# FP4 weight preparation with ScalarE's part in it, and a later place for the NF4 LoRA product

## The reference, cut to what matters

```python
def _lin_lora(x, W, A, B):            # NF4 block; W = NF4[codes] * scales per 64
    base = einsum('bsh,oh->bso', x, W)
    lora = einsum('bsr,or->bso', einsum('bsh,rh->bsr', x, A), B)
    return base + lora

def nvfp4_qdq(x, select_num):         # FP4 block; for w_gate, w_up, w_down and activations
    s = maximum(max(abs(x)) / (448.0 * 6.0), 1e-12)
    xb = (x / s).reshape(..., D // 16, 16)
    sb = clip(max(abs(xb), axis=-1) / 6.0, 1e-12, 448.0)
    a = xb / sb
    q = sign(a) * FP4_LEVELS[digitize(abs(a), FP4_BOUNDS)]   # 0, .5, 1, 1.5, 2, 3, 4, 6
    dq = (q * sb).reshape(x.shape) * s
    return where(arange(D) >= D - select_num, x, dq)         # the last 128 stay
```

## Time and profile before

| what | us |
|---|---|
| runs of the kernel | 823.1, 827.39, 827.72; median 827.39 |
| the profiled execution, its own time | 826.83 |
| its span | 825.5 |
| busy in the span: TensorE, VectorE, ScalarE, GpSimd | 725.4, 569.2, 443.6, 191.4 |
| mean granted TensorE clock | 0.957 |

### The profile page before, as it was taken

The page is one execution under the profiler, slowest core; times in us unless marked ns, Lnnn a source line. Parts: engine busy times, 40 slices in busy tenths (PEclk is TensorE's granted clock), DMA queues, the critical chain, the costliest instruction groups (busy, mean ns, idle before and its releaser), DMA issues.

```text
span 825.5 us, 11308 instructions
## 1 busy us (share of the span) xinstructions
PE 725.4 (88%) x4136; PEld 539.0 (65%) x4136; DVE 569.2 (69%) x1083; ACT 443.6 (54%) x575; POOL 191.4 (23%) x176
## 2 busy tenths in 40 slices
PE   2798765988999998889998998788999899959998
PEld 1565522656777766667665777576777688947886
DVE  4779966553597788879897986468463434477773
ACT  4778876556767767877765712255322211224542
POOL 0204000022263542534555444112201100000000
PEclk9999956999999999999998999999999999978999
DMA  7636688776366676758766111211301110200001
GB/s 280 223 107 216 206 260 266 234 246 197 125 200 205 200 240 208 227 170 265 231 178 186 65 38 43 57 28 50 90 0 36 36 52 10 77 1 13 25 26 39
DMA packets 56039, 110.55 MB, mean 134 GB/s; under 512 B 9888, under 2 KB 20800, under 8 KB 55984
## 3 DMA queue, kind: packets, MB, share of 16 engines
q1 hardware_dynamic: 42560, 78.43, 29.9%
q10 hardware_dynamic: 9040, 17.30, 6.4%
q0 software_dynamic: 4384, 14.09, 5.9%
HBM read 91.65 MB, written 18.15 MB: 133 GB/s over the span
## 4 chain that ended last, share of the span: by engine, by line
PE 52%; DVE 21%; ACT 10%; issue 9%; DMA 6%; SPq 1%; ACTq 1%; POOL 0%; DVEq 0%; POOLq 0%
PE bank L1130 13%; PE bank L1131 13%; PE bank L1132 13%; ACT hot L1537 3%; PE bank L1238 3%; DVE x L1906 2%; DVE hot L1783 2%; DMA wide_buf<-in_down_flat 2%; DVE bank L1809 2%; ACT c L1496 2%; PE bank L1426 2%; PE bank L1280 1%; PE bank L1251 1%; DVE q_a L1856 1%; DMA codes<-c 1%
## 5 line engine op out<-in xcount | busy, mean ns | idle before, releaser
L1537 ACT ACTIVATE hot<-rep,levels 128x2048 f16<-128x2048 f16 x96 | 193.6, 2057 | 18.2 <-ACT c L1496 11.1
L1130 PE MATMUL bank<-zt_h,w_h 128*128 128x512 f32 (+1 forms) x232 | 93.2, 402 | 2.5 <-DVE zt_l L1894 2.0
L1132 PE MATMUL bank<-zt_h,w_l 128*128 128x512 f32 (+1 forms) x232 | 91.3, 394 | 0.0
L1131 PE MATMUL bank<-zt_l,w_h 128*128 128x512 f32 (+1 forms) x232 | 91.2, 393 | 0.0
L1238 PE MATMUL bank<-hot,diag 128*32 128x512 f16 x1160 | 78.6, 401 | 2.2 <-ACT hot L1537 2.2
L1130 PE MATMUL bank<-w_h,xq_h 128*128 128x512 f32 (+1 forms) x192 | 74.4, 387 | 5.2 <-DVE w_l L1925 3.0
L1131 PE MATMUL bank<-w_l,xq_h 128*128 128x512 f32 (+1 forms) x192 | 72.0, 375 | 0.0
L1132 PE MATMUL bank<-w_h,xq_l 128*128 128x512 f32 (+1 forms) x192 | 71.9, 374 | 0.0
L2050 POOL TENSOR_TENSOR q_a<-q_a,q_m 128x384 f32<-128x384 f32 (+3 forms) x34 | 35.7, 1050 | 107.6 <-DVE q_m L1677 106.9
L2106 POOL TENSOR_TENSOR at_l<-ztok,at_h 128x512 fp32r<-128x512 f32 x28 | 37.4, 1336 | 80.8 <-ACT at_h L1569 80.7
L1238 PEld LDWEIGHTS bank<-hot,diag 128*32 128x32 f16 x1160 | 26.3, 99 | 45.6 <-issue 24.3
(11 more groups left out here) (222 smaller groups left out, 1688.8 us busy)
## 6 DMA issues: line engine op xcount, KB each, us to landing
rep<-codes SPq DMA_DIRECT2D x58, 512.0 KB
codes<-c SPq DMA_DIRECT2D x29, 256.0 KB
raw<-in_codes_gu_t ACTq DMA_DIRECT2D x14, 512.0 KB
sc<-in_scales_gu_t SPq DMA_DIRECT2D x56, 128.0 KB
raw<-in_codes_attn_t ACTq DMA_DIRECT2D x8, 512.0 KB
raw<-in_codes_down_t ACTq DMA_DIRECT2D x7, 512.0 KB
sc<-in_scales_down_t SPq DMA_DIRECT2D x28, 128.0 KB
wide_buf<-in_gate_flat SPq DMA_DIRECT2D x5, 512.0 KB, 4.5
```

The lines of the kernel that those rows point to most:

```text
L1130: PE.matmul(psum, lh, rh, start=first, stop=False, **kw)
L1131: PE.matmul(psum, lh, rl, start=False, stop=False, **kw)
L1132: return PE.matmul(psum, ll, rh, start=False, stop=last, **kw)
L1537: S.activation(hots[plan.slot[hot_ring(t), (t, m)]][:], codes_in_place(t), ACT.Relu, bias=bias, scale=slope).then_inc(sem("ramp_act"), 1)
```

## The change

In `make_plan`: for jobs after the attention ones, `lora(t-1)` is no longer emitted behind `look(t)` in step t, but first thing in step t+1, ahead of `high_part(t-1)`. For FP4 groups: `wround` on VectorE ends with the product, into which the enlargement of the reciprocal is folded; a new step `wlarge` one yield later has ScalarE make the absolute value times 2^22 as bf16 and copy the kept columns; a new step `wlimit`, one further yield later and just ahead of the next group's `wround`, has VectorE raise that to its least value (bf16) and then GpSimd add and subtract; `wfinish` comes one yield behind `wlimit`. The store on SP also waits for `wlarge`, and a turn bank with kept columns is free when `wlarge` is done.

```diff
@@ make_plan
     def high_parts():
+        while scaled:
+            lora(scaled.pop(0))
         while unsettled:
             p.add("high_part", unsettled[0])
             halved.append(unsettled.pop(0))
...
                 assemble(t - 1)
-                lora(t - 1)
+                if i < n_attn:
+                    lora(t - 1)
+                else:
+                    scaled.append(t - 1)
...
+def has_kept(name, c, o):
+    return name != "down" or c == len(CHUNKS) - 1
...
             def turn(o):
-                p.add("wturn", name, c, o)
-                turn_bank(("w", name, c, o), ("dve", "wread", name, c, o))
+                key = name, c, o
+                p.add("wturn", *key)
+                turn_bank(("w", *key), ("dve", "wround", *key), *[("act", "wlarge", *key)] * has_kept(*key))
...
+                limited = large
+                if limited:
+                    p.add("wlimit", *limited)
                 p.add("wround", name, c, o)
-                p.note("wread", name, c, o)
                 p.take("q_tmp", 2, ("w", name, c, o), ("dve", "wfinish", name, c, o))
                 p.take("q_out", 2, ("w", name, c, o), ("dma", ("wstored", name, c, o)))
                 yield
-                if pending:
-                    finish(pending)
-                pending = (name, c, o)
+                large = name, c, o
+                p.add("wlarge", *large)
+                if limited:
+                    finish(limited)
                 yield
-        finish(pending)
+        p.add("wlimit", *large)
+        finish(large)
@@ act_program
+            elif kind == "wlarge":
...
+                act.wait_ge(*done("dve", "wround", *key))
+                last = S.activation(um.bitcast(BF16)[0:orow, 0:nq], ua[0:orow, 0:nq], ACT.Abs, scale=2.0 ** 22)
+                if nq < w:
+                    for m in vacant("q_out", ("w", *key)):
+                        act.wait_ge(*m)
+                    if name == "down":
+                        act.wait_ge(*landed("idx"))
+                        last = S.activation(out_tile[:, nq:w], bank[:, nq:w], ACT.Copy, scale=mscale[:, o:o + 1])
+                    else:
+                        last = S.copy(out_tile[0:orow, nq:w], bank[0:orow, nq:w])
+                last.then_inc(sem("wlarge_act"), 1)
@@ dve_program, wround (magic() is gone)
-                reciprocals(rb, cb)
-                ins = V.tensor_tensor(blocks_of(ua, nq), blocks_of(src, nq), spread_of(rb, orow, nq), ALU.mult)
...
-                magic(ua, um, nq).then_inc(sem("wround_dve"), 1)
-                if nq < w:
...
-                        ins = V.tensor_scalar(out_tile[:, nq:w], bank[:, nq:w], mscale[:, o:o + 1], None, ALU.mult)
...
-                        ins = V.tensor_copy(out_tile[0:orow, nq:w], bank[0:orow, nq:w])
+                steady.up(V.reciprocal(rb, cb))
+                steady.wait_ge()
+                ins = V.scalar_tensor_tensor(blocks_of(ua, nq), blocks_of(src, nq), A_LITTLE_MORE,
+                                             spread_of(rb, orow, nq), ALU.mult, ALU.mult)
+                ins.then_inc(sem("wround_dve"), 1)
+            elif kind == "wlimit":
...
+                dve.wait_ge(*done("act", "wlarge", *key))
+                V.tensor_scalar(um, um, LEAST_LARGE, None, ALU.max).then_inc(sem("wlimit_dve"), 1)
             elif kind == "wfinish":
-                dve.wait_ge(*done("pool", "wround", *key))
+                dve.wait_ge(*done("pool", "wlimit", *key))
@@ pool_program
-            elif kind == "wround":
+            elif kind == "wlimit":
...
-                round_off(ua, um, nq, done("dve", "wround", *key), own).then_inc(sem("wround_pool"), 1)
+                round_off(ua[0:orow, :], um.bitcast(BF16)[0:orow, :], nq, done("dve", "wlimit", *key), own).then_inc(
+                    sem("wlimit_pool"), 1)
@@ sp_program, wfinish
                 sp.wait_ge(*done("dve", "wfinish", *key))
+                sp.wait_ge(*done("act", "wlarge", *key))
```

More of the change, by code:

```diff
@@ L33 @@
 LEAST_LARGE = 1.5 * 2.0 ** 22
+A_LITTLE_MORE = 1.0 + 2.0 ** -22
 NF4 = np.array([-1.0, -0.6961928009986877, -0.5250730514526367, -0.39491748809814453, -0.28444138169288635,
@@ L273, in make_plan @@
     p.jobs, p.n_attn, p.last_of = jobs, n_attn, last_of
-    through, made, unsettled, halved = {None}, [0], [], []
-    p.turns = 0
+    through, made, scaled, unsettled, halved = {None}, [0], [], [], []
+    p.turns, p.settles = 0, []
     def turn_bank(key, *freed_by):
@@ L416, in until @@
         if any(t // CU <= i for t in unsettled):
+            p.settles.append(i)
             high_parts()
@@ L462, in fp4_weights @@
         yield
-        pending = None
+        large = None
         for n, (name, c) in enumerate(STREAM):
@@ L1545, in act_program @@
                 S.copy(weight_of(j)[0][:, j["k0"] + t % 2, :], look_bank(t)[:]).then_inc(sem("made_act"), 1)
+            elif kind == "wlarge":
+                name, c, o = key
+                orow, w, nq = wround_size(*key)
+                ua, um, _, _ = q_tmp[plan.slot["q_tmp", ("w", *key)]]
+                bank, out_tile = turn(("w", *key)), q_out[plan.slot["q_out", ("w", *key)]]
+                act.wait_ge(*done("dve", "wround", *key))
[9 more added lines that the diff above has]
+                last.then_inc(sem("wlarge_act"), 1)
             elif kind == "merge":
@@ L1662, in reciprocals @@
             steady.wait_ge()
-            steady.up(V.tensor_scalar(r, r, 1.0 + 2.0 ** -22, None, ALU.mult))
+            steady.up(V.tensor_scalar(r, r, A_LITTLE_MORE, None, ALU.mult))
             steady.wait_ge()
@@ L1838, in dve_program @@
                 bank = turn(("w", *key))
-                ua, um, cc, rr = (v[0:orow, :] for v in q_tmp[plan.slot["q_tmp", ("w", *key)]])
-                out_tile = q_out[plan.slot["q_out", ("w", *key)]]
+                ua, _, cc, rr = (v[0:orow, :] for v in q_tmp[plan.slot["q_tmp", ("w", *key)]])
                 src, cb, rb = bank[0:orow, :], cc[:, 0:nq // FP4_BLOCK], rr[:, 0:nq // FP4_BLOCK]
@@ L1854, in dve_program @@
                 steady.wait_ge()
-                reciprocals(rb, cb)
-                ins = V.tensor_tensor(blocks_of(ua, nq), blocks_of(src, nq), spread_of(rb, orow, nq), ALU.mult)
[L1857 to L1862, removed]
-                magic(ua, um, nq).then_inc(sem("wround_dve"), 1)
-                if nq < w:
-                    for m in vacant("q_out", ("w", *key)):
-                        dve.wait_ge(*m)
-                    if name == "down":
-                        ins = V.tensor_scalar(out_tile[:, nq:w], bank[:, nq:w], mscale[:, o:o + 1], None, ALU.mult)
-                    else:
-                        ins = V.tensor_copy(out_tile[0:orow, nq:w], bank[0:orow, nq:w])
-                    ins.then_inc(sem("wread_dve"), 1)
+                steady.up(V.reciprocal(rb, cb))
[4 more added lines that the diff above has]
+            elif kind == "wlimit":
+                orow, w, nq = wround_size(*key)
+                um = q_tmp[plan.slot["q_tmp", ("w", *key)]][1].bitcast(BF16)[0:orow, 0:nq]
+                dve.wait_ge(*done("act", "wlarge", *key))
+                V.tensor_scalar(um, um, LEAST_LARGE, None, ALU.max).then_inc(sem("wlimit_dve"), 1)
             elif kind == "wfinish":
@@ L1982, in dve_program @@
                 steady.wait_ge()
-                V.tensor_scalar(inv_lo, inv_lo, 1.0 + 2.0 ** -22, None, ALU.mult).then_inc(sem("floor_dve"), 1)
+                V.tensor_scalar(inv_lo, inv_lo, A_LITTLE_MORE, None, ALU.mult).then_inc(sem("floor_dve"), 1)
             elif kind == "scale":
@@ L2098, in pool_program @@
                                ("gather", *key))
-            elif kind == "wround":
+            elif kind == "wlimit":
                 orow, w, nq = wround_size(*key)
-                ua, um, _, _ = (v[0:orow, :] for v in q_tmp[plan.slot["q_tmp", ("w", *key)]])
-                round_off(ua, um, nq, done("dve", "wround", *key), own).then_inc(sem("wround_pool"), 1)
+                ua, um, _, _ = q_tmp[plan.slot["q_tmp", ("w", *key)]]
+                round_off(ua[0:orow, :], um.bitcast(BF16)[0:orow, :], nq, done("dve", "wlimit", *key), own).then_inc(
+                    sem("wlimit_pool"), 1)
             elif kind == "gu_mul":
```

5 lines of the change are left out of this document (removed).

## The result

| kernel | median us | runs | against before |
|---|---|---|---|
| before | 826.25 | 823.1 to 827.72 (4) | |
| changed | 839.01 | 834.79 to 841.11 (4) | 1.0138, 95% interval 1.0108 to 1.0167 |

The ratio with its interval is the estimate on record; the quotient of the two medians would be 1.0154. The profiled execution of the changed kernel took 841.11 us (span 839.8), 14.3 more than that of before.

The account below looks back on a forecast made before the run. TensorE was taken as nearly full, VectorE's lateness showing where the order makes TensorE wait. Terms -14 - 1.5 - 2 + 9 + 1.5 + 2.7 + 1 = -3.3 us against 826.83 gave 823.5, forecast 824; 8-in-10 range 808 to 839.

Parts of the forecast that it names:

- The place of the new wait: Transposes on TensorE wait for a bank that ScalarE's wlarge frees behind its ramps: four places, +9 us (0 to +15).
- GpSimd's lateness: Rounding started behind the gathers makes wfinish wait 8 us over four chunks; a third reaches TensorE: +2.7 us (0 to +8).
- The ramps: TensorE's 2.2 us of waits for ScalarE's ramps grow by +1.5 us (0 to +8).
- part 1: The LoRA product one step later: all twelve TensorE waits for the scaled tile, 16.2 us, could go.
- -14: Gain in us taken for moving the LoRA product, out of 16.2 us of TensorE waits (bounds -16.2 and -8).
- what is late next: ScalarE's high part waits for the moved product, with its queue and VectorE's low part and hits behind; ScalarE's 3.2 us lead goes.
- -1.5 of bank waits: VectorE's relief shortens TensorE's 2.9 us of waits for banks not emptied: -1.5 us (0 to -2.9).
- -2 of clock: Fewer TensorE pauses bring back some of 7.4 us of work run at the low clock: -2 us (0 to -7).
- the bound of -8: Smallest gain for moving the LoRA product, half of 16.2 us, if a late VectorE is only met by the next matmul.
- VectorE's relief: VectorE sheds 41.6 us of removed instructions, takes on 8.5 us for wlimit: 33 of its 250.6 us less.
- The shared port: VectorE's block scale behind wlimit may be blocked by GpSimd's add: by the rule 17 us of VectorE, sum some 1.5 us higher.
- The slower rival: ScalarE sets the pace at high_part, tied to TensorE in some 34 steps: +11.5 us, 838; chance 0.23.

Follow-up runs that it names:

- lora_only: The kernel before with only the LoRA product moved one step later: 828.62 us, ratio 1.0009 to the kernel before.
- cols_early: The changed kernel with ScalarE's copy of the kept columns as its own step, one yield ahead of the Abs: 830.73 us, ratio 1.0053 to the kernel before.
- fp4_only: The changed kernel with the LoRA product back at its old place: 827.82 us, ratio 1.0004 to the kernel before.
- fp4_only_kept: The changed kernel with the LoRA product at its old place and the kept columns copied on VectorE: 824.70 us, ratio 0.9972 to the kernel before.

## Why the prediction was wrong, by its own steps

- **The place of the new wait** was right: "9" us at the transposes against 10.7 measured, four places against five, and at the three that were worked out 1.5, 3.3 and 2.3 us against 1.5, 3.4 and 2.4. GpSimd's lateness: 8 us foreseen in the waits of `wfinish`, 7.0 + 2.7 measured. The ramps: 2.2 + 1.5 forecast, 2.5 measured.
- **The failed step is in part 1**: "-14", and after it "what is late next", where I named the low part and the hits behind the high part and gave them no price of their own. The two terms for the main matmuls, -1.5 of bank waits and -2 of clock, failed with it. I added up the distances from each matmul's start to the next in both traces, between the look of tile 22 (at 193 us in both) and the first add of the last block (at 520 and 534 us), by kinds of the two neighbours:

```
us, before -> changed       steps around looks and LoRA product   48.2 -> 38.4    -9.8
                            main matmul to transposes              4.9 -> 15.9   +11.0
                            main matmul to main matmul           216.7 -> 227.7  +11.0
                            everything else                                       +3.2
                            sum                                  324.4 -> 339.9  +15.4
```

  The moved product gave 9.8, not 14, and the main matmuls, for which I had put -3.5, cost 11.0: this is the largest miss of the sum. Their number is the same, 875 or 876 steps. Some 4.6 us of the 11.0 are in steps of over half a us, 3.3 in steps of 0.43 us (19 before, 35 after; most take 0.23), the rest in short delays of 0.1 us. In `lora_only` the same sum gives 225.6 for them, 8.9 of the 11.0, there mostly in the long steps, with 11.7 us of waits for VectorE's adds. The wait that VectorE's lateness caused had only moved one station on, and the bound of -8 that I gave for that was too narrow: the whole gain went.
- **The clock** was to give back 2 us and took some 5. In the stretch of that sum the granted clock was 0.984 before and 0.970 after, and the missing share times the length is 5.2 us of TensorE's work before and 10.2 after. The loss lies in pieces of 3.4 us at 1.2 instead of 2.4 GHz: three before, two of them back to back, and six in the changed kernel. Three of the six start at the end of the three longest waits at the transposes, 3.40 us until 276.68, 3.0 until 310.07 and 2.4 until 408.52:

```profile
276.00:279.40 3.40, 2.73 (x9) 2.37 (x10) 2.71 (x6) 0.53 (x2) 1.83 (x2) 0.50 0.47 167
310.20:313.60 3.40, 3.40 (x11) 2.78 (x11) 2.43 (x6) 0.90 (x3) 1.82 (x2) 0.50 0.16 60
409.20:412.60 3.40, 3.40 (x9) 2.65 (x8) 2.56 (x5) 0.00 (x0) 1.38 (x2) 0.51 0.48 154
```

  Each costs half of its 3.4 us, so these waits were paid once more, by some 5 us, where the forecast counted the wait alone. It is not only these waits that do it: `cols_early` has none of them and 0.969.
- **VectorE's relief** was right in size (busy 569.2 to 529.0, 40 us in the whole span; 33 forecast), and the folded constant cost nothing (0.569 us a product before and after). By itself it brought little: nothing in `fp4_only`, 0.3% in `fp4_only_kept`.
- **The shared port**: the block scale took 0.243 us in the kernel before; in the changed one, behind `wlimit`, it takes 0.519, and `wfinish` fell from 0.876 to 0.553, because GpSimd is done when it starts.

```profile
L1878 DVE TENSOR_SCALAR q_c<-q_r,gm 128x24 f32<-128x24 f32 (+3 forms) x34 | 17.7, 519 | 1.2
L1902 DVE TENSOR_TENSOR q_d<-q_a,q_c 128x384 f32<-128x384 f32 (+1 forms) x22 | 12.2, 553 | 7.2 <-POOL q_a L2071 7.0
...
L1889 DVE TENSOR_SCALAR q_m<-q_m 128x384 bf16<-128x384 bf16 (+3 forms) x34 | 8.8, 258 | 19.6 <-ACT q_d L1577 12.8 <-ACT q_m L1569 5.2 <-ACT q_d L1575 1.6
```

  34 times 0.276 are 9.4 us, where the prediction's estimate by the rule of the Trainium skill (SBUF — State Buffer, "SBUF: two separate sides") was 17. The rows agree with the rule: one block scale that met an add ended when the add did, 277.84 against 277.81.

```profile
276.90 0.91 POOL L2068 TENSOR_TENSOR q_a<-q_a,q_m 128x384 f32<-128x384 f32 x1 [8.29 <-DVE q_m L1889]
277.32 0.52 DVE L1878 TENSOR_SCALAR q_c<-q_r,gm 128x24 f32<-128x24 f32 x1
```

  Moving GpSimd's work also took the collisions away from a longer instruction, the two forms of `wfinish`: 22 times 0.323 and 12 times 0.357 us are 11.4 us. In sum the new order cost VectorE nothing at the port. The two forms before the change:

```profile
L1884 DVE TENSOR_TENSOR q_d<-q_a,q_c 128x384 f32<-128x384 f32 (+1 forms) x22 | 19.3, 876 | 0.0
L1881 DVE SCALAR_TENSOR_TENSOR q_d<-q_a,mscale,q_c 128x512 f32<-128x512 f32 (+1 forms) x12 | 12.0, 1003 | 0.0
```

  `wlimit` took 0.258 us, 0.25 forecast.
- **The slower rival** (838) had the right place, `high_part` and ScalarE's queue, but its time was right by luck: it put 10 us on the looks (ten steps of 1 us), where four waits of 2.5 us in all were measured, and took -14 in full. Its condition was wrong too: it wanted ScalarE busy above nine tenths, and 77% was enough, since ScalarE idles in front of the tie and works behind it. Weighing it at 0.21 to 0.23 rested on that share.

## What to carry to other kernels

An engine that works in order can pace a kernel at 77% busy: where an edit makes it wait, add up what is queued behind that wait up to the next thing that another engine needs, and hold it against the other engine's work in between. A wait of TensorE can cost more than its length: look at the granted clock right behind it. A wait that is taken away at one consumer of a late engine comes back at its next consumer unless the late engine itself becomes earlier; price both. And two edits that lean on the same slack must be tried together and apart, and with that slack refilled: here the same change was 1.4% slower, or, with one constant shifting 78 us of arrays to the relieved engine, 1.5% faster.

## What the runs showed of the hardware

A step of VectorE on 24 columns took 0.243 us on average and 0.519 when GpSimd's add had just started; GpSimd's own add with a bf16 second input took 0.94 us on average (34 of mixed width, L2068) against 1.05 with fp32 (L2050); with 384 columns 0.92 against 1.01. VectorE ran beside the two in a different order, so how much of it is the type is not shown. ScalarE's copy of 128 columns took 0.248 us from a matmul bank, 0.286 from SBUF. After three waits of TensorE of 3.4, 3.0 and 2.4 us the granted clock was 0.50 for 3.4 us each time, and most main matmuls started 0.43 us apart instead of 0.23.
